# Placing the token ids of row tiles 5 and 6 right behind their rows on GpSimd

## What is computed

```python
scores = jax.nn.sigmoid(x @ gate_w.T) + bias
topk_w, topk_idx = jax.lax.top_k(scores, TOPK)          # TOPK = 4, E = 16
topk_w = topk_w / (jnp.sum(topk_w, axis=-1, keepdims=True) + 1e-20)
...
z = jax.nn.silu(g) * u                                   # g, u: the token through Wg, Wu of an expert
out = jnp.einsum('eti,ehi->th', zw, Wd)                  # weighted by topk_w
out = out + jax.nn.silu(x @ Sg.T) * (x @ Su.T) @ Sd.T    # shared expert
```

## Time and profile before

| what | value |
|---|---|
| median of three runs | 677.14 us |
| profiled execution, its own time | 677.72 us |
| its span from first to last instruction | 675.9 us |
| PE busy | 662.4 us (98%) |
| PEld busy | 393.1 us (58%) |
| DVE busy | 335.7 us (50%) |
| ACT busy | 220.1 us (33%) |
| POOL busy | 175.6 us (26%) |

### The profile page before, as it was taken

How to read it: one execution, slowest core, us unless ns; L and a number is a source line. 1 busy time by engine, 2 the same in 40 slices (tenths; PEclk the granted TensorE clock), 3 DMA queues, 4 the chain that set the end, 5 groups by cost and what they waited for, 6 DMA issues and landing times.

```text
span 675.9 us, 9767 instructions
## 1 busy us (share of the span) xinstructions
PE 662.4 (98%) x2399; PEld 393.1 (58%) x2400; DVE 335.7 (50%) x875; ACT 220.1 (33%) x626; POOL 175.6 (26%) x227
## 2 busy tenths in 40 slices
PE   9999999999999999999999999999899999999994
PEld 6565444466777776777776776675344444444442
DVE  3995224534334556586766768465233333333332
ACT  5575522222344433535444463220111111111110
POOL 2366100001000000004314053465124333333244
PEclk9999999999999999999999999999999999999998
DMA  9999999331400200001104014426767749768645
GB/s 339 405 422 420 422 421 436 115 118 52 167 1 0 95 1 0 1 1 63 63 2 155 2 64 160 151 79 188 231 134 144 163 83 202 186 122 235 119 75 71
DMA packets 60404, 103.19 MB, mean 153 GB/s; under 512 B 7200, under 2 KB 32544, under 8 KB 59712
## 3 DMA queue, kind: packets, MB, share of 16 engines
q1 hardware_dynamic: 30320, 73.48, 29.5%
q0 software_dynamic: 8816, 18.00, 13.5%
q10 hardware_dynamic: 21232, 11.28, 5.9%
HBM read 46.60 MB, written 56.26 MB: 152 GB/s over the span
## 4 chain that ended last, share of the span: by engine, by line
PE 86%; DMA 4%; issue 3%; DVE 2%; ACTq 1%; ACT 1%; DVEq 1%; POOLq 1%; POOL 0%; SPq 0%
PE ps L1287 51%; PE ps L1482 12%; PE ps L1451 4%; PE ps L1467 4%; PE ps L1273 4%; DMA out<-rq,sidx 3%; PE ps L1398 3%; PE ps L1399 3%; PE ps L1408 3%; ACTq L449 1%; PE ps L1420 1%; DMA xr<-in_x 1%; PE ps L1334 1%; DVEq L1215 1%; DVE rq L980 1%
## 5 line engine op out<-in xcount | busy, mean ns | idle before, releaser
L1287 PE MATMUL ps<-kv,rq 128*128 x432 | 192.5, 594 | 3.2 <-issue 2.7
L1287 PE MATMUL ps<-zT,r 128*128 128x256 f32 (+1 forms) x552 | 132.5, 395 | 0.1
L1287 PEld LDWEIGHTS ps<-kv,rq 128*128 128x128 f32 x432 | 78.9, 190 | 90.3 <-issue 90.2
L1287 PEld LDWEIGHTS ps<-zT,r 128*128 128x128 f32 x552 | 103.4, 190 | 23.5 <-issue 10.1
L1482 PE MATMUL ps<-r 128*128 128x512 f32 x192 | 85.3, 593 | 0.0
L664 POOL DMA_INDIRECT out<-rq,sidx x36 | 56.6, 1573 | 99.3 <-DMA out<-rq,sidx 61.9
L586 POOL TENSOR_SCALAR ve<-mv 128x1 f32<-128x1 f32 x32 | 7.1, 223 | 260.5 <-DVE mv L1000 260.5
L798 ACT ACTIVATE r<-ps,snm 128x128 f32<-128x128 f32 x128 | 45.2, 365 | 59.7 <-DVE snm L1116 59.5
L1212 DVE TENSOR_TENSOR rq<-ps,rq 128x256 f32<-128x256 f32 x36 | 15.2, 423 | 97.3 <-ACT rq L850 97.3
L1482 PEld LDWEIGHTS ps<-r 128*128 128x128 f32 x192 | 35.1, 190 | 37.8 <-issue 37.8
L850 ACT ACTIVATE rq<-ps 128x256 f32<-128x256 f32 x36 | 13.8, 383 | 122.2 <-PE ps L1287 122.2
(11 more groups left out here) (183 smaller groups left out, 844.2 us busy)
## 6 DMA issues: line engine op xcount, KB each, us to landing
slot_rows<-rq SPq DMA_DIRECT2D x4, 8192.0 KB, 50.5
kv<-in_experts SPq DMA_DIRECT2D x54, 256.0 KB, 4.5
rq<-slot_rows ACTq DMA_DIRECT2D x138, 64.0 KB
r<-in_Wq SPq DMA_DIRECT2D x1, 3072.0 KB, 20.6
r<-in_Wo SPq DMA_DIRECT2D x2, 1536.0 KB, 6.6
r<-in_ctx SPq DMA_DIRECT2D x8, 256.0 KB, 8.2
xr<-in_x SPq DMA_DIRECT2D x8, 256.0 KB, 8.4
second_norm_rows<-zrow SPq DMA_DIRECT2D x8, 256.0 KB, 2.1
```

The source lines that it names most:

```text
L1287: mm = pe.matmul(out, lhs(k), rhs(k), start=(k == 0), stop=(k == n - 1))
```

## The change

GpSimd's program gets another order. Ids of tiles 0 to 3 follow their rows as before, and ids of tile 4 still follow the root of tile 6. The ids of tile 5 now follow the rows of tile 5 and stand ahead of the root of tile 7; the ids of tile 6 follow the rows of tile 6 and stand ahead of the rows of tile 7; the ids of tile 7 follow the rows of tile 7. So the order becomes: root 6, ids 4, rows 5, ids 5, root 7, rows 6, ids 6, rows 7, ids 7. No DMA is added or removed, and no other engine's program changes.

```diff
                 elif step[0] == "ln_stat":
                     root(J * step[1] + step[2])
-                    if step[1] == 3 and step[2] >= J - 2:
-                        place_ids(step[2] - 2)
+                    if step[1:] == (3, J - 2):
+                        place_ids(J - 4)
...
-                    if j < J - 4:
+                    if j != J - 4:
                         place_ids(j)
 
-            place_ids(J - 2)
-            place_ids(J - 1)
             for k in range(TOPK):
                 pool.wait_ge(s_sc[k], 16 * J)
```

## The result

The changed kernel takes 680.94 us (median of 11 runs, 678.83 to 687.01) against 677.75 for the kernel before in the same session (11 runs, 676.71 to 680.07). The ratio is 1.0059, with a 95% interval of 1.0039 to 1.0079: slower by 0.6%, where 676.0 was forecast. Its profiled execution is one of the longest of its runs, 686.48 us with a span of 684.7. Two lines fewer stand ahead of the code, so L1285, L811 and L1197 here are L1287, L813 and L1199 of before.

A forecast was written before the change was run, and what follows sets the result against it. PE was taken to bound the expert stage, leaving only gaps of 1.56 and 1.13 us. Closing the latter gave 677.72 - 1.13 = 676.6 us, with other traffic at 0 to 0.1; the median, 0.58 lower, 676.0; range 675.1 to 677.4.

The forecast's parts named there:

- What bounds the kernel, the two gaps: PE bounds the expert stage; near the change only its gaps of 1.56 and 1.13 us can yield a gain.
- The gap of 1.13 us: PE behind the ids' transposes: three register loads held up by the table wait; an earlier read closes it, -1.13 us.
- POOL's order and the landings: On POOL: rows 7 stay at 453.46, last id DMA starts at 462.31, table read at 468.3 to 471.3 instead of 477.27.
- POOL's order, part by part: On POOL: each four moved id DMAs take 5.05 us, ids 5 fit into idle time, and waits cost nothing.
- Rival (c): Rows of tile 7 come late on POOL and block 2's gap grows one for one: 678.6 us, chance 0.05.
- block 2's gap: PE's 1.56 us ahead of block 2's gate_up, waiting on its rows' DMA; only DMA load could touch it.
- What the other traffic does: Table read meets block 2's row load on the DMA engines: delay 0 to 0.1 us, 0.34 kept for the range.
- Does the gain last: At step 6's transposes, scatters leave room for 0.80 us of the shift; the full 1.13 is taken.
- rival (a): Gap closes but the scatter chain or something later gives the gain back: gain 0 to 0.5, 676.9 us, chance 0.17.
- the prediction's own signs of being wrong: Loads still right at the transposes' end, read still near 477, or a new gap between 497 and 515 us.
- The drain: Ahead of the scatters, 8.3 us long, seemingly of its own length; beginning some 8 us earlier, it brings the first scatter forward 0.7.
- The sum: Whole kernel: 677.72 - 1.13 = 676.6 for the profiled execution, 0.58 less for the median: 676.0 us.

The follow-up runs named there:

- e7: Kernel before, POOL untouched, with PE's three register loads taken ahead of its wait for the table of ids; 678.32 us, ratio 1.0001.
- e16: Changed order with a fixed pause of some 3 us on GpSimd between rows and ids of tiles 5, 6 and 7; 675.98 us, ratio 0.9970.
- e18: Kernel before in its own order, with fixed pauses between ids 5 and rows 6 and between rows 7 and ids 6; 684.60 us, ratio 1.0102.
- e8: Changed order, ids of tiles 5 to 7 written by plain instead of indirect DMAs to an unread table, without routed experts; 675.10 us, ratio 0.9951.

## Why the prediction was wrong

**What bounds the kernel, the two gaps: right.** The gap of 1.13 us belongs to the register loads held up by the wait for the table. e7 removes it by moving the loads, e16 by an earlier read; in e18, with a later read, it is 1.32, and PE waits 4.15 us for the table besides.

**POOL's order and the landings: right where signals were on time.** In e16 ids 5 fit into the idle stretch even with a pause. In the changed kernel the read started at 469.01, where 468.3 to 471.3 was forecast, but two errors cancel in that: the last id DMA started 2.1 us late (464.44 for 462.31) and landed in 4.6 us, where 5.9 was taken.

**The price of the moved DMAs, "POOL's order, part by part": the step that failed.** The prediction priced them by POOL's own time (5.05 us for four, put into an idle stretch) and by their waits, which it said "cost nothing". What their issue does to PE, ACT and DVE is a term that it put at nothing without a reason: it asked only who waits for POOL. e16 has the same DMAs in the same order, broken up by pauses, and takes 5 us less than the changed kernel; so the unbroken strings cost some 5 us, over four times the gain of 1.13. The move joined ids 4, rows 5 and ids 5 to a string of 15.0 us and rows 6 to ids 7 to one of 20.3 us, where before the strings were 9.9, 9.9 and some 12. G then fell 11.8 us into a string, P 7.2, S 10.8 and T, by its time in before, over 17; before, G fell outside and S 1.7 us into one.

**Rival (c) was on the right side with the wrong mechanism.** Rows 7 did start late, at 455.59, by 2.1 us, but POOL lost only 0.4 us in the eight DMAs ahead of them (445.07 to 455.59): these started 2.2 us late, since the slots of tile 6 came late, for want of G. And a delay of rows 7 isn't what cost most: block 2's gap didn't grow, it vanished, since PE itself was later than the load. Nor does the price that (c) gave hold, each us of delay as one us of gap: in e16 rows 7 start 2.5 us later than before (455.93), and the gap is 1.57 for 1.56.

**What the other traffic does: 0 to 0.1 fits, as far as it was tested.** In e16 the read comes into block 2's load, at 475.30, and the gap is 1.57 against 1.56. The 0.34 us which the round of queues would have given, by the rule in the Trainium skill, "DMA: Bandwidth & Descriptors", section "Queues, rings and completion order", doesn't show there. But DVE turns block 2's rows at 477.19 in e16, so only some 1.9 us of the read can have met their load there.

**Does the gain last: in e16 yes, in the changed kernel not.** Step 6's transposes are at 507.01 in e16, 1.33 us earlier than in the earlier trace rows; 0.8 to 1.1 was forecast. The first scatter is at 488.09 instead of 488.46. In the changed kernel 2.3 us are given back between 487 and 524 us, with the gap of 0.71 us ahead of 520.69. That is the chain of rival (a), and one of the prediction's own signs of being wrong, a new gap between 497 and 515 us by the clock of before. The drain took 6.3 us in e16 and 6.0 in the changed kernel, not 8.3, so it had no length of its own.

**The sum.** That 676.0 is the time of e16 (675.98) is in part luck. The kernel before took 677.82 in that session, so e16 gains 1.8 us where the sum has 1.13, and it has pauses that nobody forecast. Between the two traces 1.33 us are won by step 6 and another 0.4 only near 632 us, which the prediction doesn't have. The chance for slower, 0.07, was far too small. (By its own terms faster is 0.25, not 0.26.) The range was drawn from the costs that the trace of before could show. Its one execution had P and T on time; in the three other traces with the same ids 5 and rows 6, P was late.

## What to carry to other kernels

Where an engine's program is a long string of DMAs that it issues itself, count the unbroken length of the string and look at which small, chained signals of other engines fall into its late part. Moving DMAs into an engine's idle time can be worse than leaving them, since the idle time may have been the break, as it was here. If a trace shows waits with a remote releaser, or chained small operations of one engine that pause for 1 us each, as these did, try a pause in the string of the neighbour before anything else. And look at more than one execution: a spread of 9 us among runs of one kernel, when the next has 1, is itself a finding.

## What the runs showed of the hardware

- Signals between PE, ACT and DVE came 2 to 7 us late in 20 of 23 cases in which GpSimd had issued indirect DMAs for over 8 us without a break, and 1 to 2.4 us late in 2 of 27 at most 1.4 us into a string or outside one. A fourth signal, due 10.8 us into strings of 20.3 us, came 12.2 to 12.3 us late in all three such traces. A pause of 2.5 to 2.8 us was enough; one of 1.0 to 1.4 us was enough in two traces of four.
- It isn't bytes or pieces: 128 pieces of 8 or of 64 bytes and 16 pieces of 8 bytes did the same, plain DMAs from the same engine in the same places didn't. DMA engines were at 22% in the worst stretch. Whether the length of the string in time counts, the number of its DMAs or the number not yet landed, the runs don't separate.
- What holds the signals isn't known. The Trainium skill, "DMA: Bandwidth & Descriptors", section "SWDGE vs HWDGE vs iDMA", says that GpSimd writes the descriptions of its DMAs into rings which the DMA engines drain. A ring or a path that fills up after some six or seven DMAs and empties at the string's end would fit the delays; no run here shows one, and e8, whose plain DMAs come from GpSimd too, would need an explanation of its own.
- A register load on PE's sequencer cost nothing where the sequencer was ahead of the array (474.3 us) and about 0.65 us where it wasn't; three of them behind a late wait left a gap of 1.13 us in before and 1.32 us in e18.
